# A Trainium2 kernel of sliding-window attention, test-time memory and top-2 experts: the end of attention, the opening of the gradient and the turn to merge rearranged

## What is computed

```python
x_in = concat([mem (64 rows), layernorm(x)])
q, k, v = x_in @ wq.T, x_in @ wk.T, x_in @ wv.T          # 4 heads of 64
logits = where(j <= i and j > i - 128, q k^T / 8, -1e30)  # window of 128
out_swa = (softmax(logits) v) @ wo.T
# gradient of 0.5 * sum((mlp(x_in) - out_swa) ** 2), mlp(x) = silu(x @ w1.T + b1) @ w2.T + b2
upd = (1 - alpha) * p - theta * grad(p)       for p in (w1, b1, w2, b2)
out_mem = mlp(upd, x_in)
x1 = x + sigmoid(out_swa @ lin1.T) * out_swa + sigmoid(out_mem @ lin2.T) * out_mem
out = x1 + top-2 of 8 experts (256 -> 1024 relu -> 256, capacity limited) of layernorm(x1)
```

## Time and profile before

| | us |
|---|---|
| median of 3 runs | 2405.83 (2405.38 to 2406.82) |
| the profiled execution, whole | 2407.89 |
| its span in the profile | 2406.1 |
| PE busy | 2341.6 (97%) |
| DVE, ACT, POOL busy | 1689.2, 1603.1, 1399.7 |
| attention ends, gradient starts | 454.1 |
| gradient ends, merge starts | 1410.2 |

### The profile page before, as it was taken

One profiled execution on the slowest core, in us unless ns is written; L12 is line 12 of the kernel. 1 busy time (PEld: TensorE's weight loads), 2 busy tenths in 40 slices (PEclk: granted clock), 3 DMA queues, 4 the chain that ended last, 5 costly groups with the idle time before them and its releaser, 6 DMA issues. The chain is left out here.

```text
span 2406.1 us, 39918 instructions
## 1 busy us (share of the span) xinstructions
PE 2341.6 (97%) x14802; PEld 2080.7 (86%) x14802; DVE 1689.2 (70%) x3661; ACT 1603.1 (67%) x2439; POOL 1399.7 (58%) x1002
## 2 busy tenths in 40 slices
PE   7999999799999999999999989999999999999998
PEld 6888888688888888888888978777777789999998
DVE  6787776466666666666666676777777757777776
ACT  4788888657777777777777646666766645554453
POOL 3565566556767776666767734666666553333433
PEclk9999999899999999999999999999999999999999
DMA  4222221532232332222233322332222165555551
GB/s 128 82 89 71 89 79 54 205 124 62 62 69 66 77 62 62 65 64 62 63 70 64 88 91 80 102 104 95 86 85 83 31 144 148 147 136 152 147 141 58
DMA packets 295393, 221.73 MB, mean 92 GB/s; under 512 B 189282, under 2 KB 262023, under 8 KB 295072
## 3 DMA queue, kind: packets, MB, share of 16 engines
q1 hardware_dynamic: 281376, 188.74, 29.2%
q0 software_dynamic: 13824, 30.44, 4.2%
HBM read 113.30 MB, written 72.12 MB: 77 GB/s over the span
## 5 line engine op out<-in xcount | busy, mean ns | idle before, releaser
L2653 ACT ACTIVATE e_hf<-e_ps_z,e_b 128x640 f32<-128x640 f32 x128 | 101.8, 795 | 214.1 <-PE e_ps_z L105 213.6
L2380 POOL TENSOR_TENSOR m_hl<-m_hf,m_hh 128x512 fp32r<-128x512 f32 x112 | 157.6, 1412 | 104.8 <-ACT m_hh L1983 103.4
L2780 POOL DMA_INDIRECT out<-e_ys,slot_token x80 | 83.2, 1040 | 217.9 <-DVE e_ys L2732 212.4
L105 PE MATMUL e_ps_y<-r_w_h,e_hl 128*128 128x256 f32 x640 | 180.3, 282 | 0.1
L105 PE MATMUL e_ps_y<-r_w_l,e_hh 128*128 128x256 f32 x640 | 178.8, 279 | 0.0
L105 PE MATMUL e_ps_y<-r_w_h,e_hh 128*128 128x256 f32 x640 | 178.7, 279 | 0.0
L1569 POOL TENSOR_TENSOR halves_l<-hT_full,halves_h 128x512 fp32r<-128x512 f32 x120 | 153.5, 1301 | 38.7 <-ACT halves_h L1229 38.7
L844 POOL DMA_INDIRECT xbuf_d<-xn,scatter_rows x128 | 147.3, 1151 | 41.8 <-issue 38.6
L701 POOL TENSOR_TENSOR prob<-prob,softmax_small 128x1024 f32<-128x1024 f32 x65 | 123.1, 1894 | 71.6 <-DVE softmax_small L634 71.6
L105 PE MATMUL e_ps_z<-slotsT_h,w_l 128*128 128x320 f32 x512 | 159.5, 311 | 0.5 <-DVE slotsT_l L2710 0.5
L105 PE MATMUL e_ps_z<-slotsT_l,w_h 128*128 128x320 f32 x512 | 159.4, 311 | 0.0
(11 more groups left out here) (342 smaller groups left out, 9034.9 us busy)
## 6 DMA issues: line engine op xcount, KB each, us to landing
shared_xT<-xT_d SPq DMA_DIRECT2D x64, 256.0 KB, 4.6
new_w1T<-in_W SPq DMA_DIRECT2D x16, 1024.0 KB, 5.1
new_w2T<-in_W SPq DMA_DIRECT2D x16, 1024.0 KB, 5.8
xbuf_d<-new_w1T SPq DMA_DIRECT2D x16, 650.0 KB, 8.0
shared_x<-in_x SPq DMA_DIRECT2D x16, 512.0 KB, 4.1
xn_d<-xn SPq DMA_DIRECT2D x32, 256.0 KB, 2.4
xT_d<-shared_xT SPq DMA_DIRECT2D x32, 256.0 KB, 2.6
oT_d<-shared_oT SPq DMA_DIRECT2D x32, 256.0 KB, 2.6
```

The costliest lines, as they stand in the source:

```text
L105: i = e.matmul(out, a, b, start=first and not onto and n == 0, stop=last and n == len(terms) - 1, skip_group_check=onto)
L2380: e.tensor_tensor(hl[:, t, 0:N], hf[(HC * C + t) % NZ][:, 0:N], hh[:, t, 0:N], ALU.subtract).then_inc(*h_low(C, t))
L2653: e.activation(hf[(HC * i + t) % NHF][:].rearrange("p (s n) -> p s n", s=2), ps_z[t % 2][:, :, 0:HALF], ACTF.Relu, bias=b1[:, i % E, t:t + ...
L2780: e.indirect_dma_start(io["out"], bass.IndirectOffsetOnAxis(ap=token[i % 2][:, b:b + 1], axis=0), ys[:, b], None, bounds_check=NT - 1, oob ...
```

## The change

1. **Last block of attention.** `round_pt` and `rest_pt` work on block 63 in two halves of 512 columns (one for each block of keys). `attend_last` goes by key block: after the first half is there, it issues 6 of the 12 products, into two different banks (`ps_av`, and `ps_scores` for the second pair of heads). The step over POOL is gone: ACT rounds from the banks directly into `attnT_h` in four pieces of 64x128 and DVE subtracts in four pieces (L709 of the changed kernel). On DVE the second subtraction for w2T (`rest_w2T(1)`) stands before them.
2. **Extra products.** `keep_busy(4)`: 4 products of 512 columns whose result nobody reads, after `attend_last` and again at the end of PE's attention queue; 12 more at the end of PE's gradient queue.
3. **Sigmoid's table** is loaded at the end of ACT's attention queue by a sigmoid of one column (`a_spare`), and not before the first sigmoid of the gradient.
4. **The last store of `oT`** is issued by SP in the gradient block, behind the load of x for pair 1, and not in the attention block.
5. **Opening of the gradient.** PE: z of pair 1's first block is multiplied between the two pairs of transposes. ACT: three sigmoids in a row, then x of pair 1 is rounded, then seeds, the fourth sigmoid, and the rounding of h and of its transposes, the transposes of a block ahead of the rounding of h for block 1. DVE: the subtraction for x of pair 1 stands before block 1's h.
6. **End of the gradient.** DVE: `fold(1)` stands before `final_backward`. POOL: the last `sum_dz` stands before `halves_l`.

Its core as a diff:

```diff
@@ attention, tensor
+            def attend_last():
+                par, at, _ = place(last)
...
+                for kb in range(2):
+                    pe.wait_ge(*last_pt_low.at(kb))
+                    for c2 in range(KC):
+                        vc = slice(c2 * P, (c2 + 1) * P)
+                        i = matmul_split(e, last_bank(c2), [(vh[par][:, at + kb, vc], vl[par][:, at + kb, vc])],
...
+            def keep_busy(n):
+                pe.wait_ge(*top_made.at(last))
...
-                if a - 3 in turns:
+                if a - 3 in turns and a - 3 < last:
                     attend(a - 3)
+                if a - 3 == last - 1:
+                    attend_last()
+                    keep_busy(4)
                 for kind, *key in late + output_at(a):
                     do[kind](*key)
+            keep_busy(4)
@@ attention, scalar
+            def round_last_av():
+                G, cols = group(last), rows_in_group(last)
+                act.wait_ge(*out_done.at(before(G), KC - 1))
+                for c in range(KC):
+                    act.wait_ge(*last_av_done.at(c))
+                    for h, r in enumerate(rows_of_half):
+                        e.activation(ah[slot(G)][r, c, cols], last_bank(c)[r, h * P:(h + 1) * P], ACTF.Copy).then_inc(*last_av_high(c, h))
...
+            act.wait_ge(*half_set.at(0))
+            e.activation(spare[:], neg_half[:, 0:1], ACTF.Sigmoid)
@@ attention, sync
-                    if m == KC - 1:
+                    if m == KC - 1 and G != NGRP - 1:
                         store_out(G)
@@ gradient, tensor
             transpose_h(0, 0)
+            forward(1, 0)
             transpose_h(0, 1)
-            forward(1, 0)
...
+            pe.wait_ge(*rest_made.at(TILES - 1, 1))
+            for _ in range(12):
+                e.matmul(banks[0][:], w2h[:, 0, 0:P], w2h[:, 0, 0:512], start=True, stop=True)
@@ gradient, scalar
-            for b in range(2):
-                forward(0, b)
-                seeds(b)
-                round_h(0, b)
+            forward(0, 0)
+            forward(0, 1, 0)
             round_xT(1)
+            seeds(0)
+            forward(0, 1, 1)
+            round_h(0, 0)
             round_hT(0, 0)
+            seeds(1)
             round_hT(0, 1)
+            round_h(0, 1)
@@ gradient, vector
             forward(0, 0)
+            rest_xT(1)
             forward(0, 1)
-            rest_xT(1)
...
+            fold(1)
             final_backward()
             for t in range(4):
                 final_w2(t)
             for t in range(4):
-                if t == 2:
-                    fold(1)
                 final_w1(t)
@@ gradient, gpsimd
+            pool.wait_ge(*final_dz_low.at(1))
+            sum_dz(TILES - 1)
             pool.wait_ge(*chunk_high.at(0))
             e.tensor_tensor(halves[1][:, 0:KC * T], shared.xT[0][:], halves[0][:, 0:KC * T], ALU.subtract)
-            pool.wait_ge(*final_dz_low.at(1))
-            sum_dz(TILES - 1)
@@ gradient, sync
             load_xT(1)
+            for h in range(2):
+                e.dma_start(io["oT_d"][2 * (NGRP - 1) + h],
+                            shared.oT[:].rearrange("p (k t) -> p k t", k=KC)[:, :, 2 * h * P:(2 * h + 2) * P]).then_inc(*oT_out(NGRP - 1, h))
```

More of the change, by code:

```diff
@@ L295, in attention_phase @@
         tx_done, qk_done, v_done, out_done = (signal(k + "_done", kinds[k]) for k in ("x", "qk", "v", "o"))
-        score_done, pt_done, av_done = (signal(n, turns) for n in ("score_done", "pt_done", "av_done"))
+        most = turns[:-1]
+        score_done, pt_done, av_done = (signal(n, t) for n, t in (("score_done", turns), ("pt_done", turns), ("av_done", most)))
+        last, rows_of_half = NBLK - 1, [slice(0, DH), slice(DH, P)]
+        last_av_done = signal("last_av_done", range(KC))
         stat_made = signal("stat_made", [(G, i) for G in groups for i in range(2)])
@@ L339, in bank, with last_bank @@
             return ps_p[turn[u] % 3]
+        def last_bank(c2):
+            return ps_av[:, 0] if c2 == 0 else ps_s[:, 1, 0]
         def freed(*u):
@@ L436, in attend @@
                 i.then_inc(*av_done(g))
+            def attend_last():
+                par, at, _ = place(last)
+                pe.wait_ge(*v_low.at(group(last), 1))
+                pe.wait_ge(*av_full.at(last - 1))
+                pe.wait_ge(*top_made.at(last))
[4 more added lines that the diff above has]
+                        i = matmul_split(e, last_bank(c2), [(vh[par][:, at + kb, vc], vl[par][:, at + kb, vc])],
+                                         [(pth[last % 2][:, kb, 2 * c2:2 * c2 + 2], ptl[last % 2][:, kb, 2 * c2:2 * c2 + 2])],
+                                         first=kb == 0, last=kb == 1)
+                        if kb:
+                            i.then_inc(*last_av_done(c2))
+            def keep_busy(n):
+                pe.wait_ge(*top_made.at(last))
+                ones = w["wq"][0]
+                for _ in range(n):
+                    e.matmul(ps_s[:, 0].rearrange("p a b -> p (a b)"), ones[:, 0, 0:P], ones[:].rearrange("p k d -> p (k d)"),
+                             start=True, stop=True)
             do = {"x": transpose_x, "qk": project_qk, "v": project_v, "o": out_project}
@@ L496, in round_pt @@
                 act.wait_ge(*av_done.at(g - 2))
+                if g == last:
+                    for kb in range(2):
+                        e.activation(pth[g % 2][:, kb], ps_pt[:, kb], ACTF.Copy).then_inc(*last_pt_high(kb))
+                    return
                 e.activation(pth[g % 2][:], ps_pt[:], ACTF.Copy).then_inc(*pt_high(g))
@@ L544, in scalar @@
                     soft(a)
-                if a - 3 in turns:
+                if a - 3 in turns and a - 3 < last:
                     copy_av(a - 3)
+                if a - 3 == last:
+                    round_last_av()
                 for kind, *key in late + output_at(a):
@@ L636, in rest_pt @@
             def rest_pt(g):
+                if g == last:
+                    for kb in range(2):
+                        dve.wait_ge(*last_pt_high.at(kb))
+                        e.tensor_tensor(ptl[g % 2][:, kb], ps_pt[:, kb], pth[g % 2][:, kb], ALU.subtract).then_inc(*last_pt_low(kb))
+                    return
                 dve.wait_ge(*pt_high.at(g))
@@ L642, in rest_w2T, with rest_last_av @@
                 e.tensor_tensor(w2Tl[:, 4 * k:4 * k + 4], xn[k][:], w2Th[:, 4 * k:4 * k + 4], ALU.subtract)
+            def rest_last_av():
+                G, cols = group(last), rows_in_group(last)
+                for c in range(KC):
+                    for h, r in enumerate(rows_of_half):
+                        dve.wait_ge(*last_av_high.at(c, h))
+                        e.tensor_tensor(al[slot(G)][r, c, cols], last_bank(c)[r, h * P:(h + 1) * P], ah[slot(G)][r, c, cols],
+                                        ALU.subtract).then_inc(*last_av_low(c, h))
             do = {"x": round_x, "qk": rest_qk, "v": rest_v}
@@ L678, in vector @@
                     norm_apply(G, j - 1)
-                if a in w2T_turns:
+                if a in w2T_turns and a - 2 < last:
                     rest_w2T(w2T_turns.index(a))
+            rest_w2T(1)
+            rest_last_av()
         def gpsimd(e):
@@ L1121, in tensor, with keep_busy @@
                 e.matmul(banks[i][:], w1h[:, 0, 0:P], w1h[:, 0, 0:512], start=True, stop=True).then_inc(*bits_set(i))
+            def keep_busy(n):
+                for _ in range(n):
+                    e.matmul(banks[7][:], w1h[:, 0, 0:P], w1h[:, 0, 0:512], start=True, stop=True)
             forward(0, 0)
```

20 lines of the change are left out of this document (14 added, 6 removed).

## The result

The changed kernel takes 2393.03 us (median of 6 runs, 2391.87 to 2394.46), the kernel before, run beside it, 2405.66 us (6 runs, 2403.37 to 2407.98): a ratio of 0.9947, with a 95% interval of 0.9938 to 0.9957. That is 12.6 us faster. The forecast was 2392.2 us, 0.8 us too low, and the time lies in its range of 2388.5 to 2399.5 us. The profiled execution took 2394.46 us, with a span of 2392.7 us.

The account below looks back on a forecast made before the run. Outside the long gradient stretch, where PE is never idle, chains over ACT, DVE and POOL and the clock after waits bound the kernel. 2.7 + 4.8 + 2.0 + 1.9 + 2.2 = 13.6 us gave 2392.2 us, range 2388.5 to 2399.5.

Parts of the forecast that it names:

- End of attention: From attention's last block to the gradient's start: the block starts at 451.4 and not at 454.1, 2.7 us gained.
- w2T's subtraction is the bound: End of attention: DVE's subtraction for w2T, queued ahead of four short ones, bounds `out_project`, which starts 1.0 us earlier.
- The rest, 1.8 us: Behind ACT's last copy of attention: table load 1.28, one-column sigmoid 0.2 and barrier 0.3 take 1.8 us, before 1.85.
- Opening, 4.8 forecast: Gradient's opening: the freed bank of `backward` comes 33.2 us into the block and not at 38.0, 4.8 us gained.
- Clock behind the opening: Behind `backward`'s freed bank: shorter PE gaps may keep full clock, worth 2.9 us or none; 2.0 us taken.
- the clock falls again at `backward`: Rival: clock holds at the turns but falls at `backward` in the gradient's opening; 11.6 us gained, 2394.2 us; chance 0.25.
- Zeros: Gradient: zeros end some 1 us later, at 44; `add_w1` comes at 42.5, covered by PE's banks; costed at nothing.
- End of the gradient, 1.9 forecast: DVE's last gradient work: `fold(0)` falls from 3.13 to 1.28 us with POOL idle; 1.9 us gained.
- Opening of merge: Merge's start: full clock instead of half, but ACT's queue becomes the bound; 2.2 us taken, between 0 and 3.0.
- The clock fell at none of the turns: Rival: the clock falls at the turns in spite of the extra products; 5.2 us gained, 2400.6 us; chance 0.10.
- DVE did stand still behind POOL: Rival: DVE doesn't stand still in the gradient's opening; 6.1 to 7.2 instead of 4.8, 2389.3 us; chance 0.12.
- No load of x was late: Slower rival: x of pair 1 lands late in the gradient's opening; each us beyond 5.8 costs one; chance 0.03.

Follow-up runs that it names:

- table loaded in the gradient: Changed kernel without the one-column sigmoid at the end of ACT's attention queue, so Sigmoid's table loads in the gradient's opening: 2391.97 us.
- table loaded earlier: Changed kernel with the one-column sigmoid moved up on ACT, directly behind its four short copies of attention: 2390.08 us.
- old opening: Changed kernel with the old order of the gradient's opening on PE, ACT and DVE, the table still loaded ahead of the block: 2399.43 us.
- longer wait: Changed kernel with two more DVE subtractions of xn of pair 1 ahead of its products for dz, lengthening PE's wait: 2396.80 us.
- without the 12: Changed kernel without the 12 extra TensorE products at the end of the gradient alone: 2394.64 us.
- POOL's waits: Changed kernel in whose gradient opening POOL waits four times for a DVE operation on SBUF alone, so as not to run beside it: 2389.57 us.
- POOL's old order: Changed kernel with `halves_l` again ahead of the last `sum_dz` on POOL at the end of the gradient: 2395.12 us.

## Why the prediction was right, point by point

**The time** was right to 0.8 us, in part by luck, because errors cancelled: too much was put down to the end of attention and to the opening, too little to merge, and 0.9 us came from stages that the change doesn't touch. The five stages that the change touches gave 12.4 us in the means of two profiles each, and 13.6 was forecast; the other 0.9 us of the 13.3 are the two stages that it doesn't touch, which moved by -0.7 and 1.6 us and do so in any kernel (from `memory_out` to the end it took 974.7 to 977.2 us in fourteen profiles).

**End of attention, 2.7 forecast, 1.7 measured** (2.4 against the first profile of before, 1.0 against the second). `out_project` started 6.91 us after the last transposed probabilities and not 7.75: 0.8 us where 1.0 was forecast, since each of DVE's short subtractions took 0.3 us and not 0.25. That w2T's subtraction is the bound was right: 0.4 us came when it was moved. The mis-sized term is the clock. The 1.5 us by which the 12 products got faster were put down to the change and its extra products. But the kernel before has this fall only in one of its two profiles, and without the extra products the clock was at 1.00 as well. The rest, 1.8 us for the load, the sigmoid and the barrier, was 1.8. It hides two effects of equal size. Without the load at that place the block starts 0.6 us after ACT's last copy (0.58 and 0.60 us in "table loaded in the gradient" and "table loaded earlier"), where it was 1.89 us in the kernel before with SP's two stores in between: moving the stores had freed 1.3 us, and the load at the end of the queue took them up again. No run moves the stores alone, so that part is argued.

**Opening, 4.8 forecast, 4.7 in the two first profiles, 4.3 in the means.** Each step of DVE's chain came where it was forecast, to 0.2 us. What the forecast left out is the fall of the clock at the barrier, from 454 to 457 us. It stands in both profiles of the kernel before, but not among the stretches that the forecast read. These are two windows and a PE row of the kernel before:

```profile
454.00:456.00 2.00, 1.84 (x4) 0.50 0.76 237
456.00:458.00 2.00, 2.00 (x8) 0.71 0.79 202
...
466.05 1.09 PE L1065 MATMUL g_bank<-g_ident,h_full 128*128 128x128 f32 x8 [2.96 <-DVE h_full L1360]
```

There it cost nothing, for PE's wait for `h_full` took it up: the transposes start 11.9 and 12.0 us into the block in the two profiles of before, and 10.8 us with the old opening, where the clock held at the barrier and the load of 1.28 us was gone: a difference no larger than the load. In the changed kernel z is on the path to x of pair 1, and such a fall costs 1.6 us. It came in 2 of the 8 profiles with the second `keep_busy(4)` and a wait of 1.5 us at the barrier, and in none of the 3 with a wait of 0.3 us. It also came in all 3 profiles with a wait of about 2.5 us there (2.53 us in both of the kernel before, 2.45 us in the one without the products). So it goes with the wait, and the products don't rule it out; whether they do more than shorten that wait isn't shown, and with these few runs the frequency is open.

**Clock behind the opening, 2.0 forecast, 2.1 measured**, 1.4 to 2.8 between single profiles. The longer wait brought the fall back, so the mechanism is shown. The rival "the clock falls again at `backward`", priced at 2.0 us, did not come where that price lies, behind the wait for the freed bank of `backward`. A fall did come earlier, between 476 and 484 us, in three of the kernels (without the 12, table loaded in the gradient, table loaded earlier). It cost nothing, since PE's wait ahead of the first product with `dpred_h` took it up: that wait shrank from 1.73 to about 0.16 us in all three. The same is not true of any fall with a wait behind it: those at the barrier and at 463 us cost 1.5 to 1.6 us although such waits followed, because they slowed products that the awaited operations themselves needed.

**Zeros**: costed at nothing, and nothing it was, though not as worked out. The forecast had the zeros end at 44 us into the block and `add_w1` wait 1.5 us under cover of PE's banks. They ended sooner: `add_w1`, at 42.3 us, did not wait for them, and where it did wait, in the kernel with POOL's waits, it started at 42.0 us. There the four banks covered a wait of 3.6 us.

**End of the gradient, 1.9 forecast, 1.9 measured.** `fold(0)` went from 3.13 to 1.27 us, and back to 3.13 with POOL's old order. The 12 products ended 0.02 us behind DVE.

**Opening of merge, 2.2 forecast, 2.5 measured** (2.1 and 2.8 against the two profiles of before; 2.2 and 2.8 in the two kernels without the products). The size was near, but the reason for taking off 0.8 us was wrong: ACT's queue didn't become the bound, and against the profile that the forecast was read from the gain was the full 2.8 us. It varies with how far half clock reaches into merge: 6.1 us in the first profile of before and 4.6 us in the second.

**The other rivals.** The clock fell at none of the turns as a whole, but at one of them now and then. DVE did stand still behind POOL in the opening; taking that away gave 3.2 us. No load of x was late: the subtraction came when ACT and POOL allowed it.

## What to carry to other kernels

Where DVE and POOL share a chain that sets the end, look for DVE operations on SBUF alone that run longer than the same operation elsewhere, and let POOL wait: four waits of POOL gave 3.2 us here. DVE then waited longer for the zeros, but TensorE was not held up. Load a table for ScalarE in a wait that the trace already shows, not at the end of the queue. Price the clock by several profiles: of the five falls that one profile showed at the changed places, one was absent in the next. A fall costs nothing where TensorE's next wait is for something that doesn't hang on the slowed products, and its full price where it does.

## What the runs showed of the hardware

- The granted clock differs between executions of one program at the same place: 1.00 in one profile of the changed kernel and 0.72 in the next from 452 to 458 us, behind the same barrier wait of 1.52 us, with 1.6 us between the two openings. Between about 41 and 55 us, where no edit reaches, the time at half clock is from some 3 to 10 us, in one or two stretches. With some 3 us of it the last transposed probabilities came at 439.2 to 439.7 us, with 10 us at 441.5 us.
- A table load on ScalarE costs its 1.28 us and no more: loaded early, it starts 0.02 us behind the copy ahead of it (445.29) and the sigmoid starts 0.02 us behind it. The copies behind it had no load of their own. The Trainium skill's drain of 1.38 us (page "ScalarE: Activation LUTs", section "What ACT_TABLE_LOAD costs") doesn't show in these rows.
- A DVE operation with two SBUF inputs ended 0.55 us (512 columns) and 1.07 us (1024 columns) after POOL's operation that it had met, as if it had only started to work then; the same operations took 0.69 and 1.28 us with POOL idle.
